# Time mixing and the head of the transformer: VectorE's batch order, three products on GpSimd, the last batch's end in later steps

## What is computed

```
rvk = layernorm(x) @ W_rvk.T ; r, v, k = split(rvk)
w = -exp(time_decay) ; u = time_first
step t:  p = max(pp, u + k_t) ; e1 = exp(pp - p) ; e2 = exp(u + k_t - p)
         y_t = (e1 * aa + e2 * v_t) / (e1 * bb + e2)
         p2 = max(pp + w, k_t) ; e1 = exp(pp + w - p2) ; e2 = exp(k_t - p2)
         aa, bb, pp = e1 * aa + e2 * v_t, e1 * bb + e2, p2
x = x + (sigmoid(r) * y) @ W_out.T
```

## Time and profile before

| what | us |
|---|---|
| runs (3): median, lowest, highest | 1766.19, 1760.12, 1773.02 |
| profiled execution: span from first to last instruction | 1761.1 |
| busy in it: TensorE, VectorE, ACT, GpSimd | 1595.8, 1448.3, 1121.4, 1047.0 |
| time mixing: first instruction to the last x_state | 0 to 103.28 |
| first matmul of the transformer | 108.64 |

### The profile page before, as it was taken

The page is one execution under the profiler, slowest core; times in us unless marked ns, Lnnn a source line. Parts: engine busy times, 40 slices in busy tenths (PEclk is TensorE's granted clock), DMA queues, the critical chain, the costliest instruction groups (busy, mean ns, idle before and its releaser), DMA issues.

```text
span 1761.1 us, 75843 instructions
## 1 busy us (share of the span) xinstructions
PE 1595.8 (91%) x32061; PEld 1276.8 (73%) x32157; DVE 1448.3 (82%) x3193; ACT 1121.4 (64%) x2014; POOL 1047.0 (59%) x1028
## 2 busy tenths in 40 slices
PE   6358999999999999999999999999999999999985
PEld 3237877778777777777777777778787777777763
DVE  8768988888888888888888888888889788888851
ACT  5226666667666667666667666667766666766652
POOL 1236766665766666666666667476667475575530
PEclk8569999999999999999999999999999999999997
DMA  2011111111111111111211111211111211011110
GB/s 84 30 31 50 36 49 36 57 42 47 32 48 36 57 42 44 34 48 31 62 42 38 40 45 30 60 36 51 40 36 39 60 36 47 27 43 51 28 41 13
DMA packets 41078, 74.97 MB, mean 43 GB/s; under 512 B 9472, under 2 KB 22568, under 8 KB 40744
## 3 DMA queue, kind: packets, MB, share of 16 engines
q1 hardware_dynamic: 40744, 70.12, 13.7%
HBM read 20.08 MB, written 2.10 MB: 13 GB/s over the span
## 4 chain that ended last, share of the span: by engine, by line
PE 73%; issue 9%; DVE 5%; ACT 4%; POOL 2%; ACTq 0%; DVEq 0%; POOLq 0%
PE bank L1258 8%; PE bank L1292 8%; PE bank L1359 8%; PE wide L1330 7%; PE bank L1248 7%; PE bank L1250 6%; PE bank L1249 6%; PE bank L1345 6%; PE bank L1414 4%; PE bank L1310 3%; PE bank L1282 2%; PE bank L1402 2%; PE bank L1404 1%; PE bank L1403 1%; ACT L1175 1%
## 5 line engine op out<-in xcount | busy, mean ns | idle before, releaser
L816 POOL TENSOR_TENSOR qk<-qk,rnorm 128x512 f32<-128x512 f32 x384 | 401.2, 1045 | 348.9 <-DVE rnorm L965 348.9
L808 POOL TENSOR_TENSOR qk<-qk,qk_sin 128x512 f32<-128x512 f32 x384 | 491.3, 1279 | 181.2 <-DVE qk_sin L928 180.9
L1107 ACT ACTIVATE squares<-bank 128x512 f32<-128x512 f32 x384 | 229.5, 598 | 162.2 <-DVE qk_sin L928 162.1
L938 DVE TENSOR_REDUCE norm<-squares 128x8 f32<-128x512 f32 x384 | 258.5, 678 | 30.7 <-ACT squares L1107 28.5
L1248 PE MATMUL bank<-w_hi,xs_hi 128*128 128x512 f32 x576 | 264.2, 459 | 13.1 <-ACT squares L1107 7.0
L921 DVE TENSOR_TENSOR qk<-bank,tables 128x512 f32<-128x512 f32 x384 | 261.9, 682 | 7.8 <-PE bank L1250 5.2
L928 DVE TENSOR_TENSOR qk_sin<-bank,tables 128x512 f32<-128x512 f32 x384 | 261.6, 681 | 0.6 <-POOL qk L808 0.6
L1258 PE MATMUL bank<-ident,qk 128*128 128x128 f32 x1536 | 237.3, 278 | 2.8 <-POOL qk L816 2.0
L1250 PE MATMUL bank<-w_hi,xs_lo 128*128 128x512 f32 x576 | 230.1, 400 | 0.0
L1249 PE MATMUL bank<-w_lo,xs_hi 128*128 128x512 f32 x576 | 228.7, 397 | 0.0
L1258 PEld LDWEIGHTS bank<-ident,qk 128*128 128x128 f32 x1536 | 185.4, 141 | 50.4 <-POOL qk L816 2.5
(11 more groups left out here) (169 smaller groups left out, 2718.0 us busy)
## 6 DMA issues: line engine op xcount, KB each, us to landing
v<-v SPq DMA_DIRECT2D x96, 390.0 KB, 3.5
v<-v SPq DMA_DIRECT2D x72, 130.0 KB, 3.7
w_raw<-in_L_ffn_Wqkv SPq DMA_DIRECT2D x36, 256.0 KB, 3.8
w_o_s<-in_L_ffn_Wo SPq DMA_DIRECT2D x6, 512.0 KB, 5.9
w_raw<-in_L_ffn_W SPq DMA_DIRECT2D x6, 341.0 KB, 5.0
mix_x_nat<-in_L_attn_x SPq DMA_DIRECT2D x4, 256.0 KB, 4.0
x_res_scratch<-mix_x_res SPq DMA_DIRECT2D x4, 256.0 KB, 2.7
w_raw<-x_res_scratch SPq DMA_DIRECT2D x4, 256.0 KB, 3.8
```

The source lines that it names most:

```text
L808: pool.tensor_tensor(qk[:, g % 2, c, :], qk[:, g % 2, c, :], qk_sin[:, (QK_CHUNKS * g + c) % SINES, :], ALU.add).then_inc(added[c], 1)
L816: pool.tensor_tensor(view, view, rnorm[:, g % 2, c * HPC:(c + 1) * HPC].unsqueeze(2) .to_broadcast([P, HPC, DH]), ALU.mult).then_inc(norme ...
L938: dve.tensor_reduce(norm2[:, c * HPC:(c + 1) * HPC], squares[:, c % 2, :].rearrange("p (h d) -> p h d", d=DH), AX.X, ALU.add).then_inc(sum ...
```

## The change

The change touches time mixing and the first two steps of the transformer.

- On VectorE, scan_maximum(0) goes ahead of the root of the other batches and of layer_norm(1) (`statistics` is split in `gather` and `spread`). Per batch the order becomes scan_state(b), residual(b - 1), scale_state(b - 2), scan_maximum(b + 1), layer_norm(b + 2), weigh_output(b), seed(b - 1), divide(b).
- f2v, f1a and num move from VectorE's weigh_output to GpSimd's new `numerator`, ahead of the split and newton; the wait of GpSimd's loop for den2 goes.
- TensorE takes centre(b - 1) first in its loop, and widen writes bank 7 in place of bank 6. ACT takes exponentials(0) ahead of batch 1's copies, and take_centred(b - 1) and exponentials(b + 1) ahead of the copies of batch b + 2.
- Batch 3 is no longer finished in the block, which ends behind rwkv(3) and scale_state(2). Its output, residual, centring, variance, root, widening and scaling become `late_...` steps in steps 0 and 1 of the transformer; the root is part of the root of step 0 (4 more columns). Their tiles lie in the tables, rows and x_state that those steps don't use yet (`LateBatch`), and what writes or reads these later gets a wait. The fourth store of x_res moves to step 1.

The core of the diff:

```
+class LateBatch:
+    def __init__(self, sem, weights, x_state, qk_rows):
+        spare = weights.tables[:, 1, :, :, :].rearrange("p k j d -> p (k j d)")
+        self.rwkv = self.xsq = spare[:, 0:SEQ]
+        self.x_res = spare[:, SEQ:2 * SEQ]
+        self.x_t = self.xc = x_state[:, BATCH - 1, :]
+        self.w_out_t = qk_rows[:, 1, 0:2, :].rearrange("p k d -> p (k d)")
+        self.o_ready, self.res_ready, self.cen_ready, self.cen_evac, self.st_ready = (
+            sem("m_" + name) for name in ("o_ready", "res_ready", "cen_ready", "cen_evac", "st_ready"))
+        self.seeded, self.bc_ready, self.xl_ready = (sem("m_" + name) for name in ("seeded", "bc_ready", "xl_ready"))
+        self.stored = [sem("m_stored0"), sem("m_stored1")]
...
-            for b in range(BATCH):
+            for b in range(BATCH - 1):
                 sp.wait_ge(res_ready, b + 1)
                 sp.dma_start(x_res_dram[:, b, :], x_res[:, b % 2, :]).then_inc(stored[b % 2], 16)
                 if b < 2:
                     weights.load(sp, w_qkv, 0, 4 + b)
-            for done in stored:
-                sp.wait_ge(done, 16 * BATCH // 2)
+            sp.wait_ge(stored[0], 32)
+            sp.wait_ge(stored[1], 16)
...
             def newton(b):
-                if not real(b):
+                if not finished_here(b):
...
+            def numerator(b):
+                p = b % 2
+                pool.wait_ge(f2_ready, b + 1)
+                pool.wait_ge(v_evac, b + 1)
+                pool.tensor_tensor(f2v[:], f2[:, p], v_s[:, p], ALU.mult).then_inc(f2v_ready, 1)
+                pool.wait_ge(f1_ready, b + 1)
+                pool.wait_ge(aa_ready, b + 1)
+                pool.tensor_tensor(f1a[:], f1[:, p], aa[:, p, 0:SEQ], ALU.mult).then_inc(f1a_ready, 1)
+                pool.wait_ge(f1a_ready, b + 1)
+                pool.wait_ge(f2v_ready, b + 1)
+                need(pool, rwkv_ready, b)
+                pool.tensor_tensor(num[:], f1a[:], f2v[:], ALU.add).then_inc(num_ready, 1)
             for c in range(2):
                 weights.split(pool, 0, c)
             pool.wait_ge(loaded_t, 16 * N_TABLE_LOADS)
             weights.make_tables(pool, 0, qk_rows, rot)
             for b in range(BATCH):
-                pool.wait_ge(den2_ready, b + 1)
+                numerator(b)
                 weights.split(pool, 0, 2 + b)
                 newton(b - 1)
...
+                need(dve, f1a_ready, b - 1)
                 dve.tensor_tensor_scan(bb[:, p, 1:], e1[:, p], e2[:, p], 0.0, ALU.mult, ALU.add).then_inc(bb_ready, 1)
...
             def weigh_output(b):
                 p = b % 2
-                dve.wait_ge(f2_ready, b + 1)
-                dve.tensor_tensor(f2v[:], f2[:, p], v_s[:, p], ALU.mult).then_inc(f2v_ready, 1)
                 dve.wait_ge(f1_ready, b + 1)
                 dve.wait_ge(bb_ready, b + 1)
                 dve.tensor_tensor(f1b[:], f1[:, p], bb[:, p, 0:SEQ], ALU.mult).then_inc(f1b_ready, 1)
-                dve.wait_ge(aa_ready, b + 1)
-                dve.tensor_tensor(f1a[:], f1[:, p], aa[:, p, 0:SEQ], ALU.mult).then_inc(f1a_ready, 1)
+                dve.wait_ge(f2_ready, b + 1)
                 dve.wait_ge(f1b_ready, b + 1)
                 dve.tensor_tensor(den[:], f1b[:], f2[:, p], ALU.add).then_inc(den_ready, 1)
-                dve.wait_ge(f1a_ready, b + 1)
-                dve.wait_ge(f2v_ready, b + 1)
-                dve.tensor_tensor(num[:], f1a[:], f2v[:], ALU.add).then_inc(num_ready, 1)
                 dve.wait_ge(er_ready, b + 1)
                 dve.wait_ge(den_ready, b + 1)
                 dve.scalar_tensor_tensor(den[:], er[:, p], 1.0, den[:], ALU.add, ALU.mult).then_inc(den2_ready, 1)
...
+                dve.tensor_tensor(rwkv_of(b), num[:], rden[:], ALU.mult).then_inc(rwkv_ready, 1)
...
+                dve.tensor_tensor(x_state[:, b, :], bank[7][:], xc[:, b % 2], ALU.mult).then_inc(xl_ready, 1)
...
             dve.wait_ge(loaded_x[0], 16)
-            statistics(0, NBLK)
+            gather(0, NBLK)
+            spread(0, NBLK)
             layer_norm(0)
-            for b in range(1, BATCH):
-                dve.wait_ge(loaded_x[b], 16)
-            statistics(NBLK, BATCH * NBLK)
-            layer_norm(1)
             dve.wait_ge(exp_dec, 1)
             dve.wait_ge(loaded_d, 32)
             seq(dve.tensor_scalar(w_neg[:], exp_decay[:], -1.0, None, ALU.mult))
+            for b in range(1, BATCH):
+                dve.wait_ge(loaded_x[b], 16)
+            gather(NBLK, BATCH * NBLK)
             scan_maximum(0)
+            spread(NBLK, BATCH * NBLK)
+            layer_norm(1)
             for b in range(BATCH):
+                scan_state(b)
+                residual(b - 1)
+                scale_state(b - 2)
+                scan_maximum(b + 1)
                 layer_norm(b + 2)
-                scale_state(b - 2)
-                scan_state(b)
-                scan_maximum(b + 1)
-                residual(b - 1)
                 weigh_output(b)
                 seed(b - 1)
                 divide(b)
-            b, p = BATCH - 1, (BATCH - 1) % 2
-            scale_state(b - 1)
-            residual(b)
-            dve.wait_ge(st_ready, b + 1)
-            seq(dve.tensor_scalar(var2[:, p], bank[7][:, 0:NBLK], EPS, None, ALU.add))
-            root(var2[:, p], rstd2[:, p], nt2[:, p], root_w[:, 0:NBLK], rs_ready)
-            scale_state(b)
-            dve.wait_ge(xl_ready, BATCH)
+            scale_state(BATCH - 2)
+            dve.wait_ge(rwkv_ready, BATCH)
+            dve.wait_ge(xl_ready, BATCH - 1)
...
+            exponentials(0)
...
+                take_centred(b - 1)
+                exponentials(b + 1)
                 take_x(b + 2)
                 take_k(b + 2)
-                exponentials(b + 1)
-                take_centred(b - 1)
                 take_vr(b + 2)
...
-                need(pe, xl_ready, b)
+                need(pe, cen_evac, 2 * b)
                 pe.matmul(bank[6][:], center[:], x_res[:, p], start=True, stop=True).then_inc(cen_ready, 1)
                 pe.wait_ge(cen_evac, 2 * b + 1)
-                need(pe, seeded, b)
+                need(pe, xl_ready, b)
...
+                centre(b - 1)
                 turn_x(b + 2)
                 project(b + 2)
-                centre(b - 1)
                 output(b)
                 widen(b - 1)
...
+                if step == 1:
+                    sp.wait_ge(late.res_ready, BATCH)
+                    sp.dma_start(x_res_dram[:, BATCH - 1, :], late.x_res).then_inc(late.stored[1], 16)
...
+                        sp.wait_ge(late.o_ready, BATCH)
                         load_rows(sp, qk_rows, q_scale, k_scale, layer_of(item) + 1, rows_loaded)
...
+                    pool.wait_ge(late.stored[1], 32)
+                    pool.wait_ge(late.xl_ready, BATCH)
                     weights.make_tables(pool, layer + 1, qk_rows, rot)
...
+                with_var = g == 0 or (t == NBLK - 1 and real(item - 1))
...
+            def late_residual():
+                dve.wait_ge(late.o_ready, BATCH)
+                dve.tensor_tensor(late.x_res, bank[5][:], late.x_t, ALU.add).then_inc(late.res_ready, 1)
+            def late_var():
+                dve.wait_ge(late.st_ready, BATCH)
+                dve.tensor_scalar(norm2[:, NORMS:], bank[7][:, 0:NBLK], EPS, None, ALU.add).then_inc(late.seeded, 1)
+            def late_state():
+                dve.wait_ge(late.bc_ready, BATCH)
+                dve.wait_ge(late.cen_evac, 2 * BATCH)
+                dve.tensor_tensor(x_state[:, BATCH - 1, :], bank[7][:], late.xc, ALU.mult).then_inc(late.xl_ready, 1)
...
                 rotate(step, 1)
+                if step == 0:
+                    late_residual()
+                if step == 1:
+                    late_state()
                 maximum(step - 2, 0)
                 maximum(step - 2, 1)
                 shift(step - 2, 0)
...
                 if t == 1:
                     finish_item(item - 2)
                 sum_squares(step, 3)
+                if step == 0:
+                    late_var()
                 normalise(step - 2, 0)
...
+            def late_centred():
+                act.wait_ge(late.cen_ready, BATCH)
+                act.activation(late.xsq, bank[6][:], ACT.Square).then_inc(late.cen_evac, 1)
+                act.copy(late.xc, bank[6][:]).then_inc(late.cen_evac, 1)
...
                 square(step, 1)
+                if step == 0:
+                    late_centred()
                 take_o(step - 3, 1)
...
+            def late_output():
+                pe.matmul(bank[5][:], late.w_out_t, late.rwkv, start=True, stop=True).then_inc(late.o_ready, 1)
+            def late_centre():
+                pe.wait_ge(late.res_ready, BATCH)
+                pe.matmul(bank[6][:], center[:], late.x_res, start=True, stop=True).then_inc(late.cen_ready, 1)
+            def late_variance():
+                pe.wait_ge(late.cen_evac, 2 * BATCH - 1)
+                for j in range(NBLK):
```

(46 more changed lines are left out.)

39 lines of the change are left out of this document (25 added, 14 removed).

## The result

The changed kernel takes **1758.25 us** (median of 18 runs, 1748.38 to 1762.5); the kernel before, run beside it, 1768.01 (18 runs, 1756.62 to 1777.69). The ratio is 0.9949, 95% interval 0.9934 to 0.9965: 9.0 us less, between 6.2 and 11.7. The profiled execution has a span of 1756.6 us and took 1758.4 with what lies around it, so it is a typical one.

The account below looks back on a forecast made before the run. TensorE was taken to bound the steady state, with VectorE fullest in time mixing, where the change acts. 0.7 + 11.4 - 3.5 = 8.6 us off gave span 1752.5, plus 5.1 for the median 1757.6 us; range 1744 to 1767.

Parts of the forecast that it names:

- The hold: Time mixing: GpSimd's work on SBUF holds VectorE's two-SBUF-input instructions for its whole length, those reading PSUM not; forecast's chance 0.70.
- e2v: VectorE instruction in time mixing that reads two SBUF tensors; in batch 2 before, it and two scans took 2.85 us.
- The rival without holds: Time mixing: tensor_tensor is not held, rwkv(3) ends at 77.3, 21.2 us off in all, 1745.0 us; chance 0.17.
- the slipping queue: Time mixing: VectorE wins each time, GpSimd's queue slips, batches take 19.0 instead of 17.2; 9.4 lost, 1767.0 us; chance 0.08.
- the end that is only moved: Steps 0 and 1: late steps wait for each other, growing them by 12.66 instead of 3.5; 1766.8 us; chance 0.05.
- Its size: Time mixing up to rwkv(3): with holds it ends at 89.9 against 90.62, a gain of 0.7 us.
- The start: Time mixing up to rwkv(0): it ends at 40.7 against 37.39, 3.3 us later.
- The batches: Time mixing, batches 1 to 3: 17.2, 17.3 and 14.7, together 49.2 us against 53.2, 4.0 gained.
- The last batch's end: Behind rwkv(3): 12.66 us go out of the block, 1.3 stay; gain 11.4 us.
- The first steps: Transformer steps 0 and 1: late steps cost 3.5 us, between 1.0 and 5.4.
- The steady state: Transformer from 134.01 us on, 1627.09 us: the change touches nothing in it that TensorE waits for.
- The sign that I set: Transformer's steady state: all is wrong if its 1627 us move by more than 5.

Follow-up runs that it names:

- the first experiment: Changed kernel with f2v, f1a and num back on VectorE and GpSimd's split again released by den2: 1758.2 us, ratio 0.9934.
- third experiment: Changed kernel with batch 3's end back in time mixing, the new order of the batches kept: 1767.05 us, ratio 0.9987.
- split released: Changed kernel with GpSimd's split waiting for den2 again, products still on GpSimd: 1759.41 us, ratio 0.9942.
- late steps later: Changed kernel with late_output behind Q1 on TensorE and late_state at the end of step 1 on VectorE: 1759.09 us, ratio 0.9944.
- all three: Changed kernel with products on VectorE, split behind den2, late_output behind Q1 and late_state at step 1's end: 1758.99 us, ratio 0.9923.
- delay: Changed kernel with fourteen more memsets on VectorE between time mixing and the transformer: 1779.03 us, ratio 1.0061.
- nine waits: Changed kernel with nine long-satisfied waits (five instructions) on TensorE behind the block's last transpose: 1758.43 us, ratio 0.9933.
- half a load, changed kernel: Changed kernel with 254 long-satisfied waits (128 instructions) on TensorE behind the block's last transpose: 1768.83 us, ratio 1.0.
- half a load, kernel before: Kernel before with 256 long-satisfied waits (128 instructions) on TensorE behind the block's last transpose: 1778.54 us, ratio 1.0065.

## Why the prediction was right

1757.6 us were forecast and 1758.25 measured, and the mechanism on which the forecast stood is there. That the number came within 0.7 us is luck: the head gained 4.2 us more than forecast, and 3.8 us behind the head, which the sum didn't have, took it back.

- **The hold: right.** Without it rwkv(3) was to end near 77.3, and the means of f1b, xd and yd were to stay at 0.69 to 0.75. They are 0.95, 1.20 and 1.17, and rwkv(3) ends at 84.96. The Trainium skill (SBUF — State Buffer, "Who interferes with whom") says the same of VectorE instructions with two SBUF inputs against GpSimd; the rows agree, at 1.75 us for e2v beside 0.67 for the x_state step that reads PSUM. The rival without holds is refuted by the rows and by the first experiment. So are the other two: the slipping queue was to make the batches 19.0 us long, and the end that is only moved was to put VectorE's first rotation of step 2 over 10 us further behind the first matmul; it came 4.9 further (121.26, so 30.29 us against 25.37).
- **Its size: too large by 4.9 us.** rwkv(3) was forecast at 89.9. The start was given 3.3 us and took 1.2 (rwkv(0) at 38.59 against 37.39): layer_norm(1) ended at 21.94, close to the 22.5 forecast, but f2v(1), charged with 1.2 us, ran under the reciprocal (from 34.47). The batches were given 17.2, 17.3 and 14.7 and took 16.23, 16.57 and 13.57. For f2v, f1a, num and the split VectorE was charged 3.8, 3.8 and 4.4 us in them. Summed over its held steps, each against its length in the earlier trace rows (layer_norm against 1.11), it lost 2.7, 3.5 and 2.2: GpSimd's instructions lay in part beside scale_state, residual and the wait for the variance, where they hold nothing. The 1.2 us for widen and scale_state in batch 2 were not needed either; x_state had no idle time.
- **The last batch's end: right.** 11.4 us forecast; 12.66 less 1.29 is 11.37. In the changed kernel's order the same end takes 11.13 (third experiment), so there its move alone is worth 9.8, and the rest comes with the order. The way from the block to the first matmul was 0.6 shorter besides (4.72 against 5.36).
- **The first steps: nearly right.** 3.5 us lost was forecast, 4.9 came in the first pair of profiles; rotate(0, 1) waited 1.56 of 1.5, and late_state cost 3.4 (2.83 of idle time and itself 0.6) where 2.9 were forecast with itself. The 1.8 us that were to be given back at step 2's first rotation did not come back in this pair: that wait is still 1.71 us. It scatters by itself, 0.35 to 2.42 in three profiles of the kernel before, none in the second of the changed one. Over three profiles of the kernel before (28.54, 27.84, 29.16) and two of the changed one (33.46, 31.60) the loss is 4.0.
- **The steady state: not in the sum.** The head gained 12.8 us (136.4, the mean of three, against 123.6, the mean of two) where 8.6 were forecast; the total gained 9.0. The sign that I set, that all is wrong if the 1627 us move by over 5, came true in the first pair (8.3). It was badly set: one kernel's own profiles differ by 7.8 and by 9.7 there.

About the 3.8 us between head and total the experiments say this much. The table sets each kernel's head against 136.4 and its total, from the ratio times 1770 us, against the kernel before; one head is one profile (the changed kernel's the mean of two), good to about 2.5 us.

| kernel | head | total (interval) | total - head |
|---|---|---|---|
| changed kernel | -12.8 | -9.0 (-11.7 to -6.2) | 3.8 |
| products on VectorE | -15.8 | -11.7 (-15.8 to -7.4) | 4.1 |
| split released | -15.3 | -10.3 (-14.5 to -6.0) | 5.0 |
| end in the block | -6.5 | -2.3 (-6.5 to 1.9) | 4.2 |
| late steps later | -15.0 | -9.9 (-14.2 to -5.8) | 5.1 |
| all three | -18.3 | -13.6 (-18.6 to -8.5) | 4.7 |
| delay | 5.7 | 10.8 (6.9 to 14.5) | 5.1 |
| nine waits | -12.3 | -11.9 (-16.6 to -7.3) | 0.4 |
| half a load, changed kernel | -0.8 | 0.0 (-4.2 to 4.2) | 0.8 |
| half a load, kernel before | 9.2 | 11.5 (6.7 to 16.3) | 2.3 |

In the first seven, TensorE's later code stands three or five instructions earlier than in the kernel before, and each loses 3.8 to 5.1 us beyond its head, however long that head is. In the last three the code stands elsewhere, and the loss is 0.4 to 2.3. That speaks against anything that depends on when the transformer starts, and would speak for the place of the code loads as the cause. But that is not shown, and the record has four things against it:

- Each difference has an interval of some 4 us to either side, and nine waits against none, the pair that differs in nothing else, is 0.9933 to 0.9949 with overlapping intervals.
- The last three kernels ran on another chip than the six experiments above them. Set against the head of the kernel before on their own chip, all three together and the delay (134.67 there) lose 3.0 and 3.4 us, the last three (137.27 there) 1.3, 1.7 and 3.2.
- The two kernels with half a load are five instructions apart, like the changed kernel and the one before. Their totals differ by 11.5 us, give or take 6, and their heads by 10.0, so no loss shows between them.
- The idle times over 1 us that end behind a packet add up to about the same: 35.3, 41.8 and 40.5 us behind the head in the kernel before, 37.5 and 41.8 in the changed one.

What the stretch behind the head does go with is the clock granted in it: over all 14 profiles it runs from 1642.9 us at a mean of 0.9816 to 1623.6 at 0.9915, with a correlation of -0.88. So the place of the loads moves the slow steps; its price in the total, and the cause of the 3.8 us, stay open.

## What to carry to other kernels

Work moved from VectorE to GpSimd is not off VectorE's path where VectorE reads two SBUF tensors at that time, nor beside layer_norm, which reads one (its four instructions of batch 1 took 2.06 us instead of 1.11): put it under a reciprocal or under steps that read PSUM, and hold back GpSimd's other work by a wait, which here was worth 4.0 us at the last batch's product and 2.5 at the first matmul. The moved products themselves earned nothing here. A chain that fills one batch's end costs little once it is spread between the steps of the next stage: 11.4 us out, 4 to 5 back. A gain of a few us at the front is to be read from the front; judge it by the total only over many runs, and after looking at whether the edit moved the code.

## What was not expected of the hardware

- **VectorE and GpSimd take turns, one instruction each.** GpSimd pays too (num 2.06 us, f2v 1.77, for 1.26), and steps on 12 columns are held like long ones: 0.65 us each against the tables, 1.17 against f2v, 0.17 alone.
- **One kernel's total goes with the granted clock of the execution.** Over 69 runs of the kernel before, the mean clock lies between 0.957 and 0.971, and the correlation with the time is -0.92: the 21 runs up to 0.960 have a median of 1775.0 us, the 12 runs from 0.967 on 1762.0. A kernel's scatter of 5 us is mostly this.
- **A wait on TensorE that is long satisfied is not free in numbers.** 128 instructions of such waits held the block's end for some 12.6 us, 0.1 us each.
